# Keys for the fourth attention made inside the third expert stage, and FFN weights turned one stage earlier

## The reference

```python
for n in range(4):
    x = x + tanh(g_xattn[n]) * attention_n(layernorm(x), ctx_768)
    x = x + tanh(g_ffn[n]) * ffn_n(layernorm(x))

# attention 3 (the fourth), 16 heads of 64
q, (k, v) = query @ w_q, split(context @ w_kv)
attn = softmax(einsum('bhqd,bhkd->bhqk', q, k) * 64**-0.5)
out = einsum('bhqk,bhkd->bqhd', attn, v) @ w_out + b_out

# ffn 2 (the third): 8 experts, top 2 per token
topk_vals, topk_idx = top_k(x @ gate_w + gate_b, 2)
comb = sum(one_hot(topk_idx) * softmax(topk_vals)[..., None])
h = gelu(einsum('btd,edf->ebtf', x, w1) + b1)
out = einsum('ebtd,bte->btd', einsum('ebtf,efd->ebtd', h, w2) + b2, comb)
```

## Time and profile before

| | |
|---|---|
| median of 3 runs | 2053.01 us (2047.53 to 2054.74) |
| the profiled execution | 2040.23 us, span 2038.5 us, mean granted TensorE clock 0.912 |
| PE busy | 1739.4 us, 85% (weight loads 1220.3, 60%) |
| DVE busy | 1320.2 us, 65% |
| ACT busy | 1277.7 us, 63% |
| POOL busy | 1170.1 us, 57% |

### The profile page before, as it was taken

The page is one execution under the profiler, slowest core; times in us unless marked ns, Lnnn a source line. Parts: engine busy times, 40 slices in busy tenths (PEclk is TensorE's granted clock), DMA queues, the critical chain, the costliest instruction groups (busy, mean ns, idle before and its releaser), DMA issues. The chain is left out here.

```text
span 2038.5 us, 55322 instructions
## 1 busy us (share of the span) xinstructions
PE 1739.4 (85%) x22173; PEld 1220.3 (60%) x22173; DVE 1320.2 (65%) x2596; ACT 1277.7 (63%) x1640; POOL 1170.1 (57%) x1089
## 2 busy tenths in 40 slices
PE   7997469999377599999999999999727839999778
PEld 3444258888266256666666666666526628888645
DVE  7874879999643675555555555554435548999765
ACT  5755358888343267777777777777515518888553
POOL 8311046666423377777777777778562336876534
PEclk9988579999689599999999999999858959999899
DMA  5232000000410200000000000000221120000000
GB/s 149 59 71 36 0 1 3 3 3 3 140 46 14 59 12 11 11 11 13 12 12 11 11 11 14 12 12 7 64 77 44 34 71 13 3 3 3 2 6 16
DMA packets 97216, 55.20 MB, mean 27 GB/s; under 512 B 43469, under 2 KB 90904, under 8 KB 96966
## 3 DMA queue, kind: packets, MB, share of 16 engines
q1 hardware_dynamic: 92662, 44.40, 8.6%
q0 software_dynamic: 3584, 6.36, 0.9%
q10 hardware_dynamic: 720, 0.92, 0.2%
HBM read 30.16 MB, written 13.75 MB: 22 GB/s over the span
## 5 line engine op out<-in xcount | busy, mean ns | idle before, releaser
L1610 POOL TENSOR_TENSOR aw_p_lo<-aw_p,aw_p_hi 128x512 f16<-128x512 f32 x512 | 576.2, 1157 | 189.2 <-issue 169.8
L1626 DVE TENSOR_REDUCE aw_max_part<-ps 128x1 f32<-128x512 f32 x512 | 351.3, 690 | 283.1 <-PE ps L1430 278.0
L1561 ACT ACTIVATE aw_p<-ps 128x1024 f32<-128x1024 f32 x256 | 260.2, 1016 | 198.8 <-PE ps L1461 196.7
L1041 POOL TENSOR_TENSOR ap_p_lo<-ap_p,ap_p_hi 128x512 f16<-128x512 f32 x256 | 290.9, 1157 | 156.4 <-issue 149.9
L1475 PE MATMUL ps<-ctx_hi_lo,aw_p_hi 128*128 128x97 f16 x2048 | 289.6, 206 | 2.1 <-POOL aw_p_lo L1610 2.1
L1477 PE MATMUL ps<-ctx_hi_lo,aw_p_hi 128*128 128x96 f16 x2048 | 288.8, 208 | 0.0
L1479 PE MATMUL ps<-ctx_hi_lo,aw_p_lo 128*128 128x97 f16 x2048 | 288.3, 205 | 0.0
L1568 ACT ACTIVATE aw_p_hi<-aw_p 128x1024 f16<-128x1024 f32 x256 | 270.9, 1058 | 8.1
L1477 PEld LDWEIGHTS ps<-ctx_hi_lo,aw_p_hi 128*128 128x128 f16 x2048 | 198.2, 97 | 25.2
L1475 PEld LDWEIGHTS ps<-ctx_hi_lo,aw_p_hi 128*128 128x128 f16 x2048 | 196.8, 96 | 11.8 <-POOL aw_p_lo L1610 4.3
L1479 PEld LDWEIGHTS ps<-ctx_hi_lo,aw_p_lo 128*128 128x128 f16 x2048 | 202.2, 99 | 0.0
(11 more groups left out here) (508 smaller groups left out, 4949.3 us busy)
## 6 DMA issues: line engine op xcount, KB each, us to landing
sf_weights_raw<-in_L_w SPq DMA_DIRECT2D x24, 256.0 KB, 4.3
slot_scratch<-x_normT SPq DMA_DIRECT2D x16, 260.0 KB, 3.8
sf_fetched<-slot_scratch SPq DMA_DIRECT2D x16, 260.0 KB, 3.0
sf_weights_raw<-in_L_w SPq DMA_DIRECT2D x8, 512.0 KB, 3.7
x_norm<-result_scratch SPq DMA_DIRECT2D x8, 256.0 KB, 4.0
aw_queries<-aw_queries SPq DMA_DIRECT2D x32, 64.0 KB, 1.9
aw_queries<-aw_q_lo SPq DMA_DIRECT2D x32, 64.0 KB, 2.0
aw_queries<-aw_queries SPq DMA_DIRECT2D x32, 36.0 KB
```

Source lines behind the costliest of these rows:

```text
L1041: nc.gpsimd.tensor_tensor(p_lo[:, i % 2, h, :], p[:, i % 2, h, :], p_hi[:, i % 2, h, :], ALU.subtract).then_inc(lo_done, 1)
L1561: nc.scalar.activation(p[:, n % 2, :].rearrange("p (b q) -> p b q", b=2), s, ACT.Exp, scale=1.0 / QS).then_inc(exp_done, 1)
L1610: nc.gpsimd.tensor_tensor(p_lo[:, n % 4, cols], p[:, n % 2, cols], p_hi[:, n % 4, cols], ALU.subtract).then_inc(lo_done, 1)
L1626: nc.vector.tensor_reduce(mpart[:, b % 2, k:k + 1], ps[:, max_bank(b, k), :], AX.X, ALU.max).then_inc(m_done, 1)
```

## The change

Three edits.

1. A set of buffers used only by the first three attentions moves from `persistent` to `passing_buffers`, opened at the start and closed after `attention_wide` of n = 2. From the freed space `M.keys` is taken: high and low tiles of [128, 24, 512] fp16.
2. In `sparse_ffn` of layer 2 TensorE makes the keys of 24 of the 32 units (three matmuls of 512 columns each, banks 4 to 6 in turn) behind the bias matmuls; ACT and DVE copy them, six at a time, after the weight copies of each of experts 4 to 7. The add to the residual moves behind them. In `attention_pairs` of n = 3 the first 48 half-steps read their keys from `M.keys`: no key matmuls, and copies 256 wide instead of 512.
3. The nine weight transposes and DVE's eight operations on them move from the start of `first_ffn` to the end of `attention_small_heads` (banks 0 to 2), and the wait for `w_read` goes.

```diff
@@ -57,11 +57,14 @@
 IC = (128, 128, 96)
+KEPT = 24
...
         M = persistent(nc, ctx)
+        passing = ExitStack()
+        passing_buffers(nc, M, passing)
         with ExitStack() as early:
@@ -72,6 +75,8 @@
                 attention_wide(nc, M, n)
+                passing.close()
+                M.keys = [ctx.enter_context(nc.sbuf_tensor(f"kept_keys_{k}", [P, KEPT, QB], F16)) for k in ("hi", "lo")]
             elif n == 1:
...
+def passing_buffers(nc, M, ctx):
...
@@ -713,6 +731,16 @@
                             max_scores(b + 2, 2 * r + 1)
+                pe.wait_ge(E.quantised, 7)
+                pe.wait_ge(exp_done, NU)
+                for j in range(6):
+                    w = IC[j % 3]
+                    nc.tensor.transpose(ps[:, j // 3, (j % 3) * P:(j % 3) * P + w], E.wn[0:w, j, :],
+                                        M.ident[0:w, 0:w])
+                for c in range(3):
+                    ins = nc.tensor.transpose(ps[0:IC[c], 2, c * P:(c + 1) * P], E.wd[:, c * P:c * P + IC[c]],
+                                              M.ident[:, :])
+                ins.then_inc(w_turned, 1)
@@ -963,6 +991,16 @@
                             quantise(step)
+                dve.wait_ge(w_turned, 1)
+                V_.tensor_copy(M.wgq[:], ps[:, 0, 0:INTER])
+                V_.tensor_copy(M.wuq[:], ps[:, 1, 0:INTER])
+                for c in range(3):
+                    V_.tensor_scalar(M.wd_hi[0:IC[c], c, :], ps[0:IC[c], 2, c * P:(c + 1) * P], WDS, None, ALU.mult
+                                    ).then_inc(w_hi, 1)
+                for c in range(3):
+                    dve.wait_ge(w_hi, c + 1)
+                    V_.scalar_tensor_tensor(M.wd_lo[0:IC[c], c, :], ps[0:IC[c], 2, c * P:(c + 1) * P], WDS,
+                                           M.wd_hi[0:IC[c], c, :], ALU.mult, ALU.subtract)
         retire(nc, sems)
@@ -1015,6 +1053,16 @@
+        kept = KEPT if W else 0
+
+        def keys_of(i, part):
+            if i // 2 < kept:
+                return M.keys[part][:, i // 2, i % 2 * SEQ:(i % 2 + 1) * SEQ]
+            return (QK_hi, QK_lo)[part][:, i % 4, SEQ:2 * SEQ]
+
+        def made(i):
+            return SEQ if i // 2 < kept else 2 * SEQ
+
         steps = range(-3, NH + 3)
@@ -1050,12 +1098,13 @@
                     s = i % 4
+                    k_hi, k_lo = keys_of(i, 0), keys_of(i, 1)
                     for kt in range(2):
-                        ks = slice(SEQ + kt * P, SEQ + (kt + 1) * P)
-                        for j, (k, q) in enumerate(((QK_hi, QK_hi), (QK_hi, QK_lo), (QK_lo, QK_hi))):
+                        ks = slice(kt * P, (kt + 1) * P)
+                        for j, (k, q) in enumerate(((k_hi, QK_hi), (k_hi, QK_lo), (k_lo, QK_hi))):
                             for h in range(2):
                                 rows = slice(64 * h, 64 * h + 64)
-                                nc.tensor.matmul(ps[:, SB + h, kt * SEQ:(kt + 1) * SEQ], k[rows, s, ks],
+                                nc.tensor.matmul(ps[:, SB + h, kt * SEQ:(kt + 1) * SEQ], k[rows, ks],
                                                  q[rows, s, 0:SEQ], start=kt + j == 0, stop=False,
@@ -1077,7 +1126,7 @@
                             ins = nc.tensor.matmul(ps[:, MB + h, t * SEQ:(t + 1) * SEQ],
-                                                   QK_hi[rows, s, t * P:(t + 1) * P], QK_hi[rows, s, SEQ:2 * SEQ],
+                                                   QK_hi[rows, s, t * P:(t + 1) * P], keys_of(i, 0)[rows, :],
                                                    start=True, stop=True)
@@ -1090,7 +1139,10 @@
                     nc.tensor.matmul(q, wq_hi[:, cols], M.xt_lo[:, sl], start=False, stop=False)
-                    nc.tensor.matmul(q, wq_lo[:, cols], M.xt_hi[:, sl], start=False, stop=True)
+                    ins = nc.tensor.matmul(q, wq_lo[:, cols], M.xt_hi[:, sl], start=False, stop=True)
+                    if made(i) == SEQ:
+                        ins.then_inc(qk_ready, 1)
+                        return
                     nc.tensor.matmul(k, wk_hi[:, cols], M.ct_hi[0:DC, sl], start=True, stop=False)
@@ -1198,7 +1250,8 @@
                         act.wait_ge(st_ready, i - 3)
-                    nc.scalar.activation(QK_hi[:, i % 4, :], ps[:, QKB, :], ACT.Copy).then_inc(qkhi_done, 1)
+                    nc.scalar.activation(QK_hi[:, i % 4, 0:made(i)], ps[:, QKB, 0:made(i)], ACT.Copy
+                                         ).then_inc(qkhi_done, 1)
@@ -1259,8 +1312,8 @@
                         dve.wait_ge(st_ready, i - 3)
-                    nc.vector.tensor_tensor(QK_lo[:, i % 4, :], ps[:, QKB, :], QK_hi[:, i % 4, :], ALU.subtract
-                                            ).then_inc(qk_done, 1)
+                    nc.vector.tensor_tensor(QK_lo[:, i % 4, 0:made(i)], ps[:, QKB, 0:made(i)],
+                                            QK_hi[:, i % 4, 0:made(i)], ALU.subtract).then_inc(qk_done, 1)
@@ -1769,18 +1821,8 @@
-                pe.wait_ge(E.quantised, 7)
-                for j in range(6):
-                    w = IC[j % 3]
-                    nc.tensor.transpose(ps[:, 4 + j // 3, (j % 3) * P:(j % 3) * P + w], E.wn[0:w, j, :],
-                                        M.ident[0:w, 0:w])
-                for c in range(3):
-                    ins = nc.tensor.transpose(ps[0:IC[c], 6, c * P:(c + 1) * P], E.wd[:, c * P:c * P + IC[c]],
-                                              M.ident[:, :])
-                ins.then_inc(w_turned, 1)
                 for q in range(NQ - 1):
                     turn_heads(q)
-                pe.wait_ge(w_read, 5)
                 for q in range(NQ - 1):
@@ -1924,16 +1966,6 @@
                 link(V.reciprocal(sig[:], sig[:]))
-                dve.wait_ge(w_turned, 1)
-                V.tensor_copy(M.wgq[:], ps[:, 4, 0:INTER]).then_inc(w_read, 1)
-                V.tensor_copy(M.wuq[:], ps[:, 5, 0:INTER]).then_inc(w_read, 1)
-                for c in range(3):
-                    V.tensor_scalar(M.wd_hi[0:IC[c], c, :], ps[0:IC[c], 6, c * P:(c + 1) * P], WDS, None, ALU.mult
-                                    ).then_inc(w_hi, 1)
-                for c in range(3):
-                    dve.wait_ge(w_hi, c + 1)
-                    V.scalar_tensor_tensor(M.wd_lo[0:IC[c], c, :], ps[0:IC[c], 6, c * P:(c + 1) * P], WDS,
-                                           M.wd_hi[0:IC[c], c, :], ALU.mult, ALU.subtract).then_inc(w_read, 1)
                 add_heads(0)
@@ -2416,6 +2448,10 @@
     TB, RB, CB, AB, GB, YB = 7, 5, 6, 0, 2, 5
+    KB = (4, 5, 6)
+    NP = LAYERS[3].H // 2
+    NK = 0 if gated else KEPT
+    wk_hi, wk_lo = M.split[3]["k"]
     ps, slots, results = M.ps, M.slots[layer], M.results
@@ -2589,10 +2626,20 @@
                     ins.then_inc(b2_ready, 1)
+
+                pe.wait_ge(owners_done, 1)
+                for j in range(NK):
+                    if j >= 3:
+                        pe.wait_ge(k_done, j - 2)
+                    qb, pair = divmod(j, NP)
+                    o, cols, sl = ps[:, KB[j % 3], :], slice(pair * P, (pair + 1) * P), slice(qb * QB, (qb + 1) * QB)
+                    nc.tensor.matmul(o, wk_hi[:, cols], M.ct_hi[0:DC, sl], start=True, stop=False)
+                    nc.tensor.matmul(o, wk_hi[:, cols], M.ct_lo[:, sl], start=False, stop=False)
+                    nc.tensor.matmul(o, wk_lo[:, cols], M.ct_hi[0:DC, sl], start=False, stop=True).then_inc(k_ready, 1)
+                if not gated:
                     pe.wait_ge(b2_done, 1)
                     pe.wait_ge(bias_done, 1)
-
-                pe.wait_ge(owners_done, 1)
+                    pe.wait_ge(k_done, NK)
                 owners = []
@@ -2693,8 +2740,16 @@
                                          ).then_inc(combT_done, 1)
+
+                def keys_high(j):
+                    act.wait_ge(k_ready, j + 1)
+                    nc.scalar.activation(M.keys[0][:, j, :], ps[:, KB[j % 3], :], ACT.Copy).then_inc(khi_done, 1)
+
                 for e in range(RING, E):
                     high(e)
+                    if NK and e > RING:
+                        for j in range((e - RING - 1) * NK // 4, (e - RING) * NK // 4):
+                            keys_high(j)
@@ -2863,15 +2918,25 @@
                     V.tensor_tensor(M.comb[:, :, 0:E], ex[:], v[:], ALU.add).then_inc(comb_done, 1)
+
+                def keys_low(j):
+                    dve.wait_ge(khi_done, j + 1)
+                    V.tensor_tensor(M.keys[1][:, j, :], ps[:, KB[j % 3], :], M.keys[0][:, j, :], ALU.subtract
+                                    ).then_inc(k_done, 1)
+
                 for e in range(RING, E):
...
                                       ).then_inc(bias_done, 1)
-                        dve.wait_ge(b2_ready, 1)
-                        xs = M.x[:].rearrange("p (b t) f -> p b (t f)", b=4)
-                        V.tensor_tensor(xs, xs, ps[:, 0:4, :], ALU.add).then_inc(b2_done, 1)
+                    if NK and e > RING:
```

(6 more changed lines are left out.)

49 lines of the change are left out of this document (28 added, 21 removed).

## The result

Over 20 runs each the changed kernel took 2037.47 us (2026.61 to 2048.76) and the kernel before 2046.13 us (2034.67 to 2061.95): ratio 0.9959, 95% interval 0.9943 to 0.9975, so 8.4 us less (5.1 to 11.7). The difference is as forecast (-9.1). It is nearer to rival 1's 2036, but rival 1's difference, -17.1, is far outside the interval. The first three of the 20 runs of the kernel before are the ones shown ahead of the prediction; the other 17 have a median of 2043.36, 5.9 above the changed kernel. On which chip or chips this comparison ran isn't known.

A forecast was written before the change was run, and what follows sets the result against it. TensorE, with an almost equally long ACT-POOL chain, was taken to bound the fourth attention, and POOL's indirect DMAs the third expert stage's scatter. Terms -7.8 + 0.9 - 2.2 = -9.1 from 2053.0 gave 2044 us; own range 2040 to 2047, wider 2034 to 2058.

The forecast's parts named there:

- rival 1: Fourth attention: TensorE alone bounds it, so removed key matmuls count in full, -15.8; total -17.1, 2036 us; chance 0.15.
- Fourth attention, -7.8: Without key matmuls, a chain through ACT and POOL limits the gain to 0.33 us per pair over 24 pairs.
- Making the keys, +0.9: Third expert stage: keys hidden behind the scatter cost 0; slower POOL issues 0.4 and a late last signal 0.5.
- a late last signal: Third expert stage: TensorE's signal for the last key may be seen late while POOL issues, 0.5 us (0 to 1.1).
- the spare: Third expert stage: keys, add and register loads ready at 1523.1, 4.7 us before the fetched rows.
- the add before 1521: Third expert stage: sign that the forecast holds, the add to the residual coming before 1521.
- The wait of the six weight copies on POOL: Third expert stage: copies for experts 5 to 7 now beside the scatter slow POOL's issues, 0.4 us (0 to 3.8).
- the bound of 3.1 for the keys' copies: Third expert stage: the keys' 24 low copies slow POOL's issues by 0, at the far end 3.1 us.
- The seam, -2.2: Between heads and first FFN: moved weight transposes and DVE operations are covered, first projection at about 198.75 instead of 201.00.
- Rival 2: Third expert stage: TensorE's signals held while POOL scatters, first turn +18.6; total +8.6, 2061.5 us; chance 0.13.
- Rival 3: Third expert stage: each key's signal 1.3 to 2.9 us late, +5.7 to +7.2; total 2049 us; chance 0.14.
- Rival 4: Fourth attention: chain doesn't get shorter, ACT or POOL set the pace; only the seam counts, 2051 us; chance 0.08.

The follow-up runs named there:

- act_dve_order: Changed kernel with ACT's high parts ahead of value/transpose copies and DVE's normalised output ahead of low copies in the fourth attention: 2060.06 us, ratio 1.0043 to the kernel before.
- before_act_order: Kernel before with ACT making the high parts ahead of the copies of values or transposes in the fourth attention: one run, 2049.91 us.
- seam_only: Kernel before with only the FFN weight transposes and DVE's operations moved to the heads' end, keys as before: 2048.54 us, ratio 0.9988.
- after_again: The changed kernel, unaltered, run once more on a third chip: 2073.06 us, ratio 1.0091 to the kernel before on that chip.

## Why the prediction was right, and where it wasn't

The difference came out within 0.7 us of the forecast, and the reason given for its largest part holds. The sum is nearer than its parts: the attention gave 0.5 us more than forecast (from the first to the last low part), the keys' making cost some 0.5 less, and the seam gave 0.9 less, so errors cancelled.

- *Fourth attention, -7.8.* Measured -7.4 by the stage and -8.3 between POOL's first and last low part (the stretch behind the last one takes 6.2 to 7.6, whichever the kernel). The reason holds: a second chain through ACT and POOL keeps 0.28 of the 0.65 that the matmuls give (a pair takes 6.89, against 7.26 before and TensorE's own 6.61), and when both orders are turned (`act_dve_order`) the rest comes. The pair was forecast at 6.94; where the other 0.05 comes from I didn't take apart. Rival 1 falls as stated. Its -15.8 is nearly reached with the two edits of order (-14.0 by the stage); ACT's is worth nothing without the keys (`before_act_order`), DVE's wasn't tried there.
- *Making the keys, +0.9.* On a free chip 0 to 0.4. The 0.5 in it for a late last signal was 0.04 (the last key's last matmul ends at 1515.59, its copy starts at 1515.62). But the spare was nearly used up. I had one key per 0.75 and the last at 1517.9, in time of the kernel before; it was 26.0 us from 1490.86 to 1516.86, so 1.08 each, and 1522.5 in that time. Three times, once in each group of six, TensorE waits 1.2 to 1.4 (the row of 1500.77), since DVE does an expert's weights there, and from 1501.7 to 1504.7 a key took 1.28, at half clock. The add ends at 1519.14; with the 2.88 of register loads this is 1522.02, against fetched rows that were turned at 1522.46: 0.4 spare, not 4.7. The sign "the add before 1521" wasn't met either: 1516.86 is 39.32 behind the first issue, 1522.5 in that time. That so short a spare sufficed was luck.
- *The wait of the six weight copies on POOL.* 40.55 against 40.44 for 32 issues, but also 40.67 in `seam_only`, where neither keys nor weight copies were moved: nothing to tell. The term 0.4 was too big, and the bound of 3.1 for the keys' copies is empty. The 1.60 that I gave as the most in the second expert stage isn't the most: an issue at 554.05 took 1.88 there.
- *The seam, -2.2.* Measured -1.8 at the projection and -1.3 at the stage's end. The term left out the clock. I took 1.84 for the nine transposes and 0.42 for the wait on DVE, and let the turns take the 2.1 that they took before. But TensorE's first 2.8 to 4.6 us in this stage run at half clock in every profile. With the transposes gone, all twelve turns fall into that stretch (2.37 from the first start to the last instead of 1.81), and that eats the 0.42; in the three other profiles without the edit the turns are slower and TensorE doesn't wait for DVE at all. Of the projection's first matmuls one to nine then start 0.21 apart instead of 0.11, which is the size of the other 0.5.
- *Rival 2, 13%.* In the timed result it did not happen, and that was luck: the profile of before showed it, and the three chips that came after the first two comparisons all had it. As a mechanism it is shown on these three, and on one of them the changed kernel was run. I took its row for a thing of one place in the program (the last signal before an idle engine) and priced it at +18.6 for the first turn, counted from the first issue. There the first turn came at 71.85 instead of 44.63 in the profile of before, so +27.2, since the second signal is late as well (7 us) and the 23 keys from there on take 1.0 each instead of 0.60 (the clock is 0.50 for the first of them and 1.00 from 1540 on); against the kernel before on the same chip, itself 5.8 late, it is +21.4. Of the two stages' difference there (236.38 less 210.79) 2.6 lies ahead of the scatter and has nothing to do with the keys. The Trainium skill's sentence in "SBUF — State Buffer", section "Who interferes with whom", that PE and ACT never wait on anyone is about SBUF ports, and the prediction was wrong to set it against this rival: TensorE's matmuls indeed weren't slowed (a key's start 0.43 apart at half clock in the free and in the held profile), its signals were late.
- *Rival 3*, each signal some us late, didn't happen: on the free chip the keys were 1.08 apart with every signal on time, on the holding one two to four signals were very late and the others weren't. *Rival 4* falls with the pair of 6.89.

## What to carry to other kernels

Work put beside another engine's long chain of indirect DMAs is hidden only if its hand-overs come through; look in every trace for a wait on an operation that had ended long before, and run the change on several chips before believing either sign. When an engine is 100% busy, look for the second chain of the same length before counting a saved instruction in full, and once that chain is seen, try the order of the engines on it. The gap at this stage's end, beside four issues instead of 32, proved the safer place.

## What the runs showed of the hardware that I had not expected

On chips (or sessions) of one kind, signals of TensorE given while POOL issues indirect DMAs arrive late: 0.5 to 3.1 us beside the four issues of a group in the second expert stage, and 13 to 32 us beside 32, for the first signal that is late. The earliest late one was given 13.6 us behind the first of the 32 issues, and one given at 6.2 us was on time. DVE saw ACT's signals at once in the same stretch (1525.12 to 1525.15 in `after_again`). On the other kind none of these was late. Nine of fourteen profiles were held: the prediction's, and eight on three further chips; the five free ones are the changed kernel's first and the four of one chip.

A second mark goes with it: of the 512 semaphore events that tell of the landing of the scatter's 32 DMAs, the free traces have 512 and the held ones 113 to 132. Whether fewer events were sent or only fewer recorded, and whether the recording of a trace has a part in the hold, no run tells. What the two kinds differ in, and why the hold starts where it does, stays open; so does whether it goes with the chip or the session, which no run here tells apart.
